# Two-layer recurrent block on one core: Wo in 32-column parts, the 16 heads' shift from weight norms, and a new order before the 16-head loop

## What is computed

```python
xn = layernorm(x)
s = attention1(xn)                     # one head of 128, Wa, Wb folded in
g = silu(mlp(xn))                      # gated 128->512, 512->512, 512->512, 512->128, ternary weights
x = x + s * g

xn = layernorm(x)
q, k, v = (xn @ Wq + bq), (xn @ Wk + bk), (xn @ Wv + bv)        # 8 heads of 64
attn = softmax(einsum('bhd,bhd->bh', q_t, k_t) / 8)             # over the 8 heads, per token
state_t = decay * state_{t-1} + (1 - decay) * attn * v_t        # decay = sigmoid(alpha)
s = layernorm((q * states + sigmoid(q * aug)) @ Wo + bo) * ln_scale + ln_bias
qkv = xn @ W_qkv + b_qkv                                        # 16 heads of 8
attn_out = softmax(q @ k.T / sqrt(8)) @ v
gate = softmax(xn @ W_gate + b_gate); combine = its top two of 8
g = silu(attn_out + sum_e combine_e * (xn @ W_experts[e] + b_experts[e]))
x = x + s * g
```

## Time and profile before

| | us |
|---|---|
| median of 3 runs | 1041.93 |
| lowest, highest | 1039.20, 1042.42 |
| the profiled execution's run | 1038.88 |
| its span in the trace | 1037.1 |
| PE busy | 972.1 (94%) |
| ACT busy | 757.4 (73%) |
| DVE busy | 560.1 (54%) |
| POOL busy | 197.7 (19%) |

### The profile page before, as it was taken

One profiled execution on the slowest core, in us unless ns is written; L12 is line 12 of the kernel. 1 busy time (PEld: TensorE's weight loads), 2 busy tenths in 40 slices (PEclk: granted clock), 3 DMA queues, 4 the chain that ended last, 5 costly groups with the idle time before them and its releaser, 6 DMA issues.

```text
span 1037.1 us, 16254 instructions
## 1 busy us (share of the span) xinstructions
PE 972.1 (94%) x6122; PEld 543.7 (52%) x6122; DVE 560.1 (54%) x1372; ACT 757.4 (73%) x926; POOL 197.7 (19%) x144
## 2 busy tenths in 40 slices
PE   3999899999899989999989989999999998999995
PEld 2888533343488843334358874334437885333431
DVE  6656634636555754654564584455447566346252
ACT  5534799989663579998955458998885346999885
POOL 1200202512300020441130002143212002025023
PEclk9999999999999999999999999999999999999998
DMA  6000132000000023100000003300000001310000
GB/s 242 1 1 1 20 50 46 1 2 1 12 11 1 1 35 49 31 1 1 2 21 1 1 2 49 64 1 1 1 1 21 2 1 17 50 26 1 1 2 22
DMA packets 14418, 20.49 MB, mean 20 GB/s; under 512 B 2848, under 2 KB 11136, under 8 KB 14080
## 3 DMA queue, kind: packets, MB, share of 16 engines
q1 hardware_dynamic: 14336, 19.41, 8.7%
HBM read 7.85 MB, written 2.10 MB: 10 GB/s over the span
## 4 chain that ended last, share of the span: by engine, by line
PE 77%; DVE 8%; ACT 6%; issue 6%; POOL 2%; DMA 0%; DVEq 0%; POOLq 0%; ACTq 0%
PE ps L1097 74%; ACT big L1053 4%; PE ps L1511 1%; DVE wk L543 1%; DVE st L277 1%; POOL st L867 1%; DVE xn L449 1%; ACT xn L1025 1%; DVE qk_max L558 1%; DVE wk L733 1%; DVE flags L417 1%; ACT qz L1001 0%; PE ps L1117 0%; PE ps L1504 0%; DVE spl L550 0%
## 5 line engine op out<-in xcount | busy, mean ns | idle before, releaser
L1053 ACT ACTIVATE big<-ps 128x1024 f32<-128x1024 f32 x512 | 493.6, 1034 | 50.8 <-PE ps L1097 48.9
L1097 PE MATMUL ps<-big,vaug 128*32 128x512 f32 x2048 | 272.6, 604 | 3.6 <-DVE wk L733 2.3
L1097 PE MATMUL ps<-hid 32*128 32x512 f32 x1024 | 130.5, 493 | 3.4 <-ACT big L1053 2.2
L1097 PE MATMUL ps<-hid,fw_sb 128*128 128x512 f32 x416 | 100.6, 396 | 0.0
L969 ACT ACTIVATE wk<-ps,cols_sb 128x512 f32<-128x512 f32 x64 | 40.5, 687 | 78.3 <-PE ps L1097 74.2
L867 POOL TENSOR_TENSOR st<-st 128x4 f32<-128x4 f32 x16 | 16.1, 1009 | 412.2 <-DVE st L532 304.1
L1097 PEld LDWEIGHTS ps<-hid 32*128 32x128 f32 x1024 | 49.1, 181 | 77.0 <-issue 41.7
L1097 PEld LDWEIGHTS ps<-hid,fw_sb 128*128 128x128 f32 x416 | 77.8, 188 | 17.6
L880 POOL TENSOR_TENSOR qz<-qz,wk 128x512 f32<-128x512 f32 x32 | 41.1, 1284 | 232.3 <-DVE wk L703 232.3
L1097 PEld LDWEIGHTS ps<-big,vaug 128*32 128x32 f32 x2048 | 41.0, 108 | 69.7 <-issue 42.3
L721 DVE SCALAR_TENSOR_TENSOR big<-ps,sm,big 128x128 f32<-128x128 f32 x128 | 44.3, 346 | 46.9 <-PE ps L1097 35.8
(11 more groups left out here) (210 smaller groups left out, 1613.7 us busy)
## 6 DMA issues: line engine op xcount, KB each, us to landing
hid<-spl SPq DMA_DIRECT2D x288, 32.0 KB
xnext<-in_x SPq DMA_DIRECT2D x4, 512.0 KB, 3.9
out<-qz SPq DMA_DIRECT2D x8, 256.0 KB, 2.3
big<-in_fw SPq DMA_DIRECT2D x1, 1877.0 KB, 9.2
wk<-in_lw SPq DMA_DIRECT2D x1, 1476.0 KB, 14.1
big<-in_fw SPq DMA_DIRECT2D x1, 939.0 KB, 11.0
cst_sb<-in_cst SPq DMA_DIRECT2D x1, 440.0 KB, 4.4
xn<-in_aw SPq DMA_DIRECT2D x1, 320.0 KB, 5.1
```

The source lines that it names most:

```text
L1053: up(ms_exp, a.activation(prob[:, at:at + 2 * CH].rearrange("p (h n) -> p h n", n=CH), ps[:, bank:bank + 2, :], ACT.Exp, scale=HDM ** -0.5))
L1097: return t_.matmul(out_, lhsT, rhs, start=start, stop=stop, **kw)
```

## The change

It has these parts. Wo: each matmul is cut into four with 32 columns of weights. eb: likewise. aT: the eight matmuls alternate between the two groups of 32 columns that they fill. The bound is made once, in batch 0, from the norms of the weights' columns (DVE squares the weights, two matmuls with ones sum them, POOL takes the root, a few small DVE steps follow; the spreading matmul stands behind the first W3 block, the five small steps behind the first `block_normalise`), and the four maxima, their steps and the matmul with ones go from every batch; so do PE's and DVE's register loads after batch 0. The fills of `k_st` by ACT become four DMAs of ones; the stack DMAs go head group by head group; POOL's fills of `q_st` no longer wait for the bound of the batch but for the second layer norm. The order of PE, ACT and DVE in the stretch is new, and banks with it. In the loop, scores begin with bank 0, cycle 0 waits for all four stacks, the sixth unit waits for the fifth product instead of the fourth stack, and ACT copies q of the sixth and seventh unit between its two exponentials instead of behind them.

```diff
-S_BANKS, S_FIRST = 6, 2
+S_BANKS, S_FIRST = 6, 0
-QK_BANKS = ((2, 3), (4, 5), (2, 3), (4, 5), (0, 1), (6, 7), (6, 7))
-MQ_BANKS = (0, 1)
-STK_BANKS = (6, 7, 6, 6)
+QK_BANKS = ((2, 3), (4, 5), (2, 3), (6, 7), (4, 5), (6, 7), (6, 7))
+MQ_BANKS = (0, 1, 1, 4)
+STK_BANKS = (0, 0, 0, 1)
+NORM_BANK, BOUND_BANK, VALUES_BANKS = 0, 3, (7, 7, 7)
...
SP
-                for j, which, first in ((1, 0, True), (1, 1, False), (0, 0, True), (0, 1, False)):
...
+                sp.wait_ge(w3_mm.sem, w3_mm.at(b, 2))
+                for g in range(GH):
+                    rows_ = slice(QUAD * g + 3 * HDM, QUAD * (g + 1))
+                    up(ones_in, sp.dma_start(k_st[rows_, 1:NG, :].rearrange("p g (a n) -> p (g a) n", n=P).bitcast(F32),
+                                             one_row[0:HDM, :].bitcast(F32).unsqueeze(1).broadcast_to([HDM, (NG - 1) * S // P, P])), 16)
+                sp.wait_ge(qfill_ok.sem, qfill_ok.at(b, NG - 1))
+                sp.wait_ge(mq_hi.sem, mq_hi.at(b, 4))
+                for g4 in range(1, NG):
+                    for j, which in ((1, 0), (0, 0), (1, 1), (0, 1)):
...
DVE, behind gate_unit(0, m)
+                if b == 0:
...
+                    done(v.tensor_tensor(squares, w_, w_, ALU.mult), "squares")
+                    done(v.scalar_tensor_tensor(qk_max[:, 2:4], biases, -1.0, biases, ALU.mult, ALU.max))
+                    v.wait_ge(setup_p, 5)
+                    done(v.tensor_scalar(norms, ps[:, NORM_BANK, 0:2], float(D), 1e-30, ALU.mult, ALU.max), "norms")
+                    v.wait_ge(norm_ok, 1)
...
DVE, the stretch
                 block_normalise(0)
+                if b == 0:
+                    v.wait_ge(bnd_mm, 1)
...
+                    need_max = v.value_load(iflag[0:1, 1:2], min_val=0, max_val=1)
                 act_units(12, 20, 1)
...
+                mq_rest(0)
                 residual(1)
                 block_stats(1)
-                mq_rest(0)
+                product(0, QK_BANKS[0][1])
                 block_normalise(1)
                 mq_rest(1)
-                product(0, QK_BANKS[0][1])
                 product(1, QK_BANKS[1][1])
-                mq_maximum(0)
-                mq_maximum(1)
                 split_rest(xt_lo, xt_hi, T_BANKS[1], 1, xT_mm, 2, x_hi, x_lo)
                 values_in(0)
-                mq_maximum(2)
-                mq_maximum(3)
...
+                product(2, QK_BANKS[2][1])
                 mq_rest(2)
...
                 mq_rest(3)
...
POOL
+                    g_.wait_ge(ln_ok.sem, ln_ok.at(b, 2))
                     up(qfill_ok, g_.tensor_tensor(q_st[:, g4, :], bias_q[:, g4:g4 + 1].broadcast_to([P, S]), one24, ALU.mult))
...
ACT
-                for g4 in range(1, NG):
-                    a.wait_ge(w3_mm.sem, w3_mm.at(b, 2))
-                    up(kfill_ok, a.activation(k_st[:, g4, :], col("row24").broadcast_to([P, S]), ACT.Copy))
+                stacked(0)
+                q_unit(2, QK_BANKS[2][0])
                 split_head(xt_hi, T_BANKS[1], 1, xT_mm, 2, x_hi)
+                stacked(1)
                 mq_head(2)
                 mq_head(3)
-                q_unit(2, QK_BANKS[2][0])
-                stacked(0)
+                q_unit(3, QK_BANKS[3][0])
                 a.activation(mrow2[:, 0:1], ones[:, 0:1], ACT.Exp)
-                q_unit(3, QK_BANKS[3][0])
-                stacked(1)
                 stacked(2)
+                stacked(3)
                 q_unit(4, QK_BANKS[4][0])
-                stacked(3)
...
PE, the stretch
                 qk_unit(0)
                 qk_unit(1)
+                stack(0)
+                t_.wait_ge(res_ok.sem, res_ok.at(b, 2))
+                values_unit(0)
+                t_.wait_ge(prod_ok.sem, prod_ok.at(b, 1))
+                qk_unit(2)
                 t_.wait_ge(ln_ok.sem, ln_ok.at(b, 2))
                 transposes(xnv, T_BANKS[1], 1)
-                values_unit(0)
-                t_.wait_ge(mq_lo.sem, mq_lo.at(b, 2))
+                t_.wait_ge(stk_ok.sem, stk_ok.at(b, 1))
+                stack(1)
                 mq_units(1)
...
-                up(bnd_mm, mm(ps[:, SIDE_BANK, 0:HM], ones, sm[:, 7, 0:HM], True, True))
...
                 qk_unit(3)
...
                 stack(2)
+                stack(3)
                 qk_unit(4)
...
PE, the loop
                     if k_ == 0:
-                        t_.wait_ge(stk_ok.sem, stk_ok.at(b, 2))
+                        t_.wait_ge(prod_ok.sem, prod_ok.at(b, 3))
+                        t_.wait_ge(stk_ok.sem, stk_ok.at(b, 4))
...
                     if what == "qk":
-                        if i == 5:
-                            t_.wait_ge(stk_ok.sem, stk_ok.at(b, 4))
-                        else:
-                            t_.wait_ge(prod_ok.sem, prod_ok.at(b, i))
+                        t_.wait_ge(prod_ok.sem, prod_ok.at(b, i))
...
-                        for t in range(NT):
+                        for t in (q_ + TPC * c_ for q_ in range(TPC) for c_ in range(NCH)):
...
-                        up(eb_mm, mm(side, ct[:, :], bexp_sb[:, i * CH:(i + 1) * CH], True, True))
+                        for g in range(GH):
+                            ins = mm(ps[QUAD * g:QUAD * (g + 1), SIDE_BANK, :], ct[:, QUAD * g:QUAD * (g + 1)],
+                                     bexp_sb[:, i * CH:(i + 1) * CH], True, True)
+                        up(eb_mm, ins)
...
                         for m in range(KM):
-                            ins = mm(side[:, q * D:(q + 1) * D], qz[:, m, c * CH + q * P:c * CH + (q + 1) * P],
-                                     wo_sb[:, m * D:(m + 1) * D], m == 0, m == KM - 1)
+                            for g in range(GH):
+                                at = c * CH + q * P + QUAD * g
+                                ins = mm(ps[QUAD * g:QUAD * (g + 1), SIDE_BANK, q * D:(q + 1) * D], qz[:, m, at:at + QUAD],
+                                         wo_sb[:, m * D:(m + 1) * D], m == 0, m == KM - 1)
```

More of the change, by code:

```diff
@@ L336, in _ @@
                     s_.given += s_.per
-                for j, which, first in ((1, 0, True), (1, 1, False), (0, 0, True), (0, 1, False)):
[L338 to L341, removed]
-                    else:
[L343 to L347, removed]
-                    for g4 in range(1, NG):
+                sp.wait_ge(w3_mm.sem, w3_mm.at(b, 2))
[7 more added lines that the diff above has]
+                    for j, which in ((1, 0), (0, 0), (1, 1), (0, 1)):
+                        dst = (q_st, k_st)[j]
+                        reps = ((0, 2), (1,))[which] if j == 0 else ((0, 1), (2,))[which]
+                        if g4 == 1 and (j, which) == (1, 1):
+                            sp.wait_ge(mq_lo.sem, mq_lo.at(b, 4))
                         for g in range(GH):
@@ L608, in _ @@
-                mq_rest(2)
-                product(2, QK_BANKS[2][1])
-                v.wait_ge(bnd_mm.sem, bnd_mm.at(b, 1))
-                bound = ps[:, SIDE_BANK, 0:HM]
-                step(v.tensor_reduce(flags[:, 1:2], bound, AX.X, ALU.min))
-                own()
-                step(v.tensor_scalar(flags[:, 2:3], flags[:, 1:2], -SAFE * HDM ** 0.5, None, ALU.is_ge))
-                step(v.tensor_scalar(iflag[:, 1:2], flags[:, 1:2], -SAFE * HDM ** 0.5, None, ALU.is_lt))
-                own()
@@ L618, in _ @@
-                step(v.scalar_tensor_tensor(bias_w[:, :].rearrange("p (a g) -> p a g", g=GH),
-                                            bound.rearrange("p (a g) -> p a g", g=GH), flags[:, 2:3], in_quad, ALU.mult, ALU.mult))
-                own()
-                up(bnd_ok, v.tensor_reduce(bias_q[:, :], bias_w[:, :].rearrange("p (a g) -> p a g", g=GH), AX.X, ALU.add))
+                product(2, QK_BANKS[2][1])
+                mq_rest(2)
                 mq_rest(3)
-                product(3, QK_BANKS[3][1])
@@ L862, in _ @@
             g_.tensor_tensor(lw_lo[:, 0:end], wk[:, 0:end], lw_hi[:, 0:end].bitcast(F32), ALU.subtract).then_inc(lw_ok, 1)
+            g_.wait_ge(setup_v, marks["norms"])
+            g_.tensor_tensor(qk_max[:, 4:6], qk_max[:, 0:2], half[:, 0:2], ALU.pow).then_inc(norm_ok, 1)
             for b in range(B):
@@ L1297, in mlp_rest @@
                             t_.wait_ge(sc_exp.sem, sc_exp.at(b, 2 * NT))
+                        elif b == 0 and m == 0:
+                            t_.wait_ge(setup_v, marks["norms"])
                         l1_unit(1, m, general)
@@ L1309, in mlp_rest @@
                     dense(FW3, D, 2, W3_BANKS[0:1], 16, general, 16, w3_mm, 1)
+                    if b == 0:
+                        t_.wait_ge(setup_v, marks["bound rows"])
+                        mm(ps[:, BOUND_BANK, 0:HM], ones, sm[:, 7, 0:HM], True, True).then_inc(bnd_mm, 1)
                     t_.wait_ge(pv_norm.sem, pv_norm.at(b, 6))
```

100 lines of the change are left out of this document (60 added, 40 removed).

## The result

The changed kernel takes **1012.97 us** (median of four runs, 1012.52 to 1013.66) against 1042.18 for the kernel before (median of four, 1039.20 to 1045.87): a ratio of 0.971, 95% interval 0.967 to 0.975. The forecast was 1014. The profiled execution's span is 1010.7 us against 1037.1, 26.4 less; I had summed up 27.8.

A forecast was written before the change was run, and what follows sets the result against it. PE's own sequence, 77% of the chain that ended last, was taken as the bound. Stretch 18.2 (with batch 0 and clock), Wo 7.0, transposes 1.8 and expert bias 0.8 sum to 27.8 off 1041.93: 1014 us, range 1007 to 1025.

The forecast's parts named there:

- Wo: 16-head loop: 32-column parts run side by side, cycle 2.52 to 2.30 us, 32 cycles, 7.0 us gained.
- (a): Rival: PE gets load/matmul pairs too slowly, 60 ns each, so a loop cycle takes 2.64; 1025 us, chance 0.10.
- (b): Rival: 89 ns is the pair rate, so 32 pairs take 2.86 us instead of 1.08; 1078 us, chance 0.04.
- the loads of 128 columns: Half of the 0.22 us gained per loop cycle: 0.11 put down to loading 128-column weights.
- The stretch: First layer's MLP end to the loop's third cycle: new order removes PE's waits, 4.8 us a batch, 19.2 in all.
- Rival (c): Before the loop: ACT or the later layer norm holds PE, half the gain, 9 us less; 1023 us, chance 0.10.
- The clock: Batches 0 and 2, before the loop: no 2.75 us stand, so no low clock after it; 1.0 us gained for both.
- Batch 0: Norm work: tiny matmuls cost PE 0.3 + 0.25, bound steps and register load delay DVE's splits 1.5; together -2.0 us.
- Expert bias: Two units a batch in the loop, cut into 32-column parts: 0.10 us each, 0.8 us gained in all.
- Attention transposes: Loop: alternating two column groups cuts unit to next scores from 1.43 to 0.97 us, four times, 1.8 us gained.
- the copies behind it move along: Attention transposes' cycle: ACT waits there, so its later copies shift earlier with PE and the 0.46 us gain is kept.
- What was to cost nothing: Four DMAs replace ACT's fills; stack DMAs begin near 370.5 us, and their new order keeps cycle 16 from waiting.

The follow-up runs named there:

- wo_fine: The changed kernel with each of Wo's matmuls cut in two of 64 streamed columns, 64 load/matmul pairs a unit: 1013.74 us.
- wo_alone: The kernel before with only Wo cut into 32-column parts: 1036.36 us, ratio 0.995 to the kernel before.
- third_back: The changed kernel with the third q and k unit again behind the second half's transposes: 1022.10 us.
- small_undone: The changed kernel with the old order of the attention transposes and the expert bias whole, as one 128-column matmul a unit: 1015.07 us.
- stack_order: The changed kernel with the 72 stack DMAs in the old order, all head groups of one part before the next: 1048.88 us.

## Why the prediction was right, step by step

**Wo, 7.0 forecast, 6.88 measured** (32 cycles, 0.215 each). Rivals (a) and (b) fell together: four column groups do run side by side when they take turns, and wo_fine puts a pair at 31 ns or less. The head sum was the right row to go by: 0.89 + 0.97 forecast, 0.88 + 0.98 measured. The Trainium skill's "TensorE: Matmul & The Clock Gate", section "Wait — 56ns, not 53.3ns?", gives 62 ns a MATMUL with hardware decode off, by which the change would have cost 6.7. This trace does not show that pace: 44 pairs in 2.30 us are 52 ns each. The advice of the Trainium skill's "TensorEngine Tiling (Array Packing)", section "Instruction Overhead", not to split what is already small did not decide here either: cutting 128 columns of weights into 32 gained 0.22 us a unit. wo_fine's cut of the streamed columns gained nothing and cost 0.02.

One thing was right in size and loose in cause: I called 0.11 "the loads of 128 columns". The single records of before have Wo's first pair at 208.146, the second at 208.359 and the others 0.112 apart, against 0.109 for 32 columns. So it is 0.10 on the first pair, and less than 0.02 on the steps behind it: both halves of the gain come once a unit, not with every load.

**The stretch, 19.2 + 1.0 forecast, 19.69 measured.** At full clock it is 4.85 and 4.83 (batches 1 and 3) for 4.8. Every step of the table above came within 0.13 us of its forecast. Rival (c), that ACT or the layer norm takes half of the gain, did not come: ACT was late, but only where I had put it, and by no more.

**The clock, 1.0 forecast, 0.7 measured.** I had both stretches about 0.5 longer. That was right for batch 0 (0.55 longer than batch 1's) and misread for batch 2 (0.16). After the change no stretch shows a low clock (a window of batch 2, of after; the other stretches read 1.00 too):

```profile
604.00:612.00 8.00, 7.05 (x28) 4.20 (x28) 5.29 (x9) 7.02 (x11) 4.92 (x3) 1.00 0.14 19
```

That is 0.7 between the two profiled executions. Between the medians more may lie in it: they are 29.2 apart and the spans 26.4, the kernel before runs from 1039 to 1046, and its profiled execution is among its fastest. This fits low clocks that come and go behind the stand, as wo_alone and third_back show; no run measured it by itself. So there is some luck in how near 1014 came: the sum of 27.8 was 1.4 too high for the spans and 1.4 too low for the medians, and no term of mine foresaw that the two would differ.

**Batch 0, -2.0 forecast, -1.96 measured, by other parts.** Up to q and k it lost 1.56 in this pair, 1.4 to 1.5 in the later runs with the same code. The places of its losses, matmul by matmul against the kernel before: 0.45 where the norm's tiny matmuls stand, another 0.2 at the matmul that spreads the bound (I had 0.3 + 0.25), and 0.8 at the last block of the MLP, which waits for DVE's splits. DVE's timeline has the reason, and below it PE's:

```profile
100.64 0.17 DVE L600 TENSOR_REDUCE flags<-ps 128x1 f32<-128x16 f32 x1
...
101.37 0.17 DVE L608 TENSOR_REDUCE bias_q<-bias_w 128x4 f32<-128x16 f32 x1
102.30 0.43 DVE L466 CAST hid<-wk 128x512 fp32r<-128x512 f32 x1 [0.76 <-issue]
```

```profile
106.70 0.73 PE L1105 MATMUL ps<-hid,fw_sb 128*128 128x512 f32 x2 [0.33 <-DVE hid L468]
...
108.48 0.73 PE L1105 MATMUL ps<-xt_lo,lw_hi 128*128 128x512 f32 x2
...
124.27 0.50 PE L1105 MATMUL ps<-hid 32*128 32x512 f32 x4 [0.88 <-issue]
124.76 0.50 PE L1105 MATMUL ps<-xt_hi,lw_hi 128*128 128x512 f32 x1
```

0.90 for the five steps as in the earlier trace rows, and the register load, which no row had timed, 0.76 for my 0.6. PE felt 0.8 of this 1.66 there, where I had put the whole on its way: in the kernel before, the last split was done at 103.88 and the matmul that takes it started at 104.89, so there was slack. A further 0.4 is lost in the stretch (21.69 for 21.29). It arises right behind the first matmuls of q and k: DVE, still late, has the low half ready later, and the two low matmuls (at 108.48) start 1.21 us after the first of q and k (at 107.27), where batch 1 has 0.94. One matmul later the lag is 0.38, and it stays up to scores 2. PE's own register load ahead of batch 0's first scores stands for 0.88 us and costs nothing in the end: scores 0 come 1.23 after their place in batch 1, but the sixth unit, which waits for product 4 in either batch, only 0.38. So the sum was right while the parts were not.

**Expert bias, 0.8 forecast, 0.46 measured: mis-sized.** Two cycles a batch gain 0.06 each, not 0.10:

```profile
166.03 1.06 PE L1105 MATMUL ps<-bexp_sb,sm 64*32 64x512 f32 x8
167.02 0.50 PE L1105 MATMUL ps<-hid 32*128 32x512 f32 x4
```

From the unit to the scores 0.99 for 1.05, but from the values to it still 1.00 (165.035 to 166.031), where Wo and the head sum with 128 rows take 0.88. Weights of 32 columns aren't enough: with 64 rows in place of 128 the form is still another, and the price of 0.11 ahead of the unit stays.

**Attention transposes, 1.8 forecast, 1.45 net measured: the step "the copies behind it move along" failed.** The cycle fell to 2.30, to the hundredth (PE's timeline, of after):

```profile
155.06 1.04 PE L1105 MATMUL ps<-cst_sb 128*32 128x128 f32 x16
156.03 0.51 PE L1105 MATMUL ps<-hid 32*128 32x512 f32 x4
```

But the next cycle grew by 0.10 in every batch. ACT's copy of the transposed attention, in before and in after:

```profile
159.70 0.59 ACT L1065 ACTIVATE sel_r<-ps 64x512 fp32r<-64x512 f32 x1 [0.39 <-PE ps L1097]
```

```profile
156.24 0.59 ACT L1073 ACTIVATE sel_r<-ps 64x512 fp32r<-64x512 f32 x1
```

Before, ACT was idle and copied 0.11 after PE's unit was over (scores at 159.59); now PE is 0.46 earlier, ACT still has an exponential in hand up to 156.22, and copies 0.21 after it (scores at 156.03). The next side unit needs the bank and so starts 0.10 later after its scores. small_undone moves that cycle back to 2.44.

The rest of the loop gave 0.3 less, most of it single cycles that scatter by 0.26 from one batch to another; I name no cause. Sum: 6.88 + 1.45 + 0.46 - 0.27 = 8.52 for 9.6 in the loop, 19.69 - 1.56 = 18.13 for 18.2 before it; less 0.36 for the start and plus 0.08 for the rest, that is the 26.4 of the spans.

**What was to cost nothing** did cost nothing: SP's stack DMAs begin at 365.31 (forecast 370.5 - 5.22 = 365.28), and no DMA holds cycle 16. That the new order is what guards it, stack_order shows.

## What to carry to other kernels

A unit whose weights have another form than its neighbours' pays at its edges, here 0.11 us behind a 32-column unit and 0.10 on its first pair; cut it into the neighbours' form, and give the column groups turns, since the same pairs group by group cost 1.38 us a unit. Before a shorter path is credited, lay out every engine's row along it from rows of the same work: what is late next is then a number, and here it also named the next gain, a table load moved to where its engine was idle. Look at what an early buffer asks of the DMA queue: an order of transfers that was harmless can become the bound.

## What the hardware showed that I had not expected

- Load/matmul pairs of four column groups follow each other at 14 ns each (wo_fine: four of 64 columns every 0.056 us), 64 pairs in 1.00 us up to the next scores.
- The same stand of PE, with the same instructions around it, is followed by full clock (1.00) in some batches and by some microseconds at 0.50 in others. Where it was low it cost 1.4 to 1.5 us more in third_back; behind the stands of 6 to 7 us in stack_order the next three cycles took 2.7 to 2.9 us more. In the changed kernel, without such stands, the runs lie within 1.1 us, those of the kernel before within 7.
- PE's register load ahead of the first scores stands 0.88 us in the changed kernel; with the table loaded early the same instruction shows no wait, and scores 0 of batch 0 come 0.96 sooner after q and k. Yet scores 2 gain there only the 0.57 of the other batches: so the 0.88 was not on the way there.
